# Attention with the transposes of the probabilities one head later, three probability buffers, and a loop over three groups

## The reference

```
q = (x @ Wq.T).reshape(B, L, HQ, HD)        # HQ, HKV, HD = 32, 8, 64; L = 512
k = (x @ Wk.T).reshape(B, L, HKV, HD)
v = (x @ Wv.T).reshape(B, L, HKV, HD)
q, k = _rope(q), _rope(k)                   # rotation of pairs of features by the position
attn = einsum('bkgqd,bkld->bkgql', qh, kh) * HD ** -0.5
p = softmax(where(causal, attn, -inf), axis=-1)
out = einsum('bkgql,bkld->bkgqd', p, vh)
x = x + out.reshape(B, L, HQ * HD) @ Wo.T
```

## Time and profile before

| | |
|---|---|
| median of 3 runs | 1674.26 us (1673.71 to 1676.47) |
| the profiled execution | 1673.25 us |
| its span, first to last instruction | 1671.5 us |
| PE busy | 1508.4 us (90%) |
| DVE busy | 1381.9 us (83%) |
| ACT busy | 1116.1 us (67%) |
| POOL busy | 1050.1 us (63%) |
| mean granted TensorE clock | 0.942 of full speed |

### The profile page before, as it was taken

The page is one execution under the profiler, slowest core; times in us unless marked ns, Lnnn a source line. Parts: engine busy times, 40 slices in busy tenths (PEclk is TensorE's granted clock), DMA queues, the critical chain, the costliest instruction groups (busy, mean ns, idle before and its releaser), DMA issues. The chain is left out here.

```text
span 1671.5 us, 31714 instructions
## 1 busy us (share of the span) xinstructions
PE 1508.4 (90%) x8951; PEld 1317.9 (79%) x8951; DVE 1381.9 (83%) x3470; ACT 1116.1 (67%) x2593; POOL 1050.1 (63%) x1161
## 2 busy tenths in 40 slices
PE   5799999999999899899899999698679999999994
PEld 4687877887778788788788878587569999999993
DVE  7898898898898898898888888377668898899882
ACT  3787877787777788788778778432146666666661
POOL 6689779779769769778778877556613322322321
PEclk9999999999999999999999999856579999999997
DMA  4000000000000000000000000111368888888775
GB/s 172 1 14 20 1 14 20 1 13 19 1 13 19 1 13 19 1 13 19 1 13 0 1 1 1 40 58 64 104 222 227 225 230 225 227 234 219 197 182 132
DMA packets 62002, 124.47 MB, mean 74 GB/s; under 512 B 20942, under 2 KB 21070, under 8 KB 61792
## 3 DMA queue, kind: packets, MB, share of 16 engines
q1 hardware_dynamic: 51408, 102.24, 19.3%
q0 software_dynamic: 10304, 20.59, 6.5%
q10 hardware_dynamic: 144, 0.07, 0.0%
HBM read 106.08 MB, written 24.71 MB: 78 GB/s over the span
## 5 line engine op out<-in xcount | busy, mean ns | idle before, releaser
L522 POOL TENSOR_SCALAR probs<-probs,row_inv 128x512 f32<-128x512 f32 (+3 forms) x512 | 282.3, 572 | 25.6 <-DVE row_inv L426 25.6
L306 ACT ACTIVATE probs<-probs,neg_max 128x512 f32<-128x512 f32 (+3 forms) x512 | 281.5, 552 | 10.2 <-DVE neg_max L419 6.5
L419 DVE CUSTOM_DVE_ANT_0 probs<-bank,causal 128x512 f32<-128x512 f32 (+3 forms) x512 | 220.6, 485 | 55.4 <-PE bank L208 42.1
L1209 POOL DMA_INDIRECT acc<-ctx_raw,idx x46 | 74.5, 1618 | 294.2 <-ACT ctx_raw L1362 279.9
L218 PE MATMUL bank<-ident,probs 128*128 128x128 f32 x1280 | 187.1, 277 | 55.5 <-POOL probs L522 38.0
L407 DVE TENSOR_TENSOR pt_lo<-bank,pt_hi 128x512 fp32r<-128x512 f32 (+1 forms) x384 | 214.8, 585 | 22.8 <-ACT pt_hi L299 22.7
L218 PEld LDWEIGHTS bank<-ident,probs 128*128 128x128 f32 x1280 | 149.8, 141 | 103.4 <-issue 48.0
L513 POOL TENSOR_TENSOR rot<-rot,sin 128x512 f32<-128x512 f32 (+1 forms) x96 | 124.0, 1291 | 165.2 <-DVE rot L438 161.8
L1290 PE MATMUL bank<-xt_hi,gu_hi 128*128 128x256 f32 x736 | 208.0, 283 | 2.0 <-DVE xt_lo L407 1.5
L1290 PE MATMUL bank<-xt_hi,gu_lo 128*128 128x256 f32 x736 | 206.2, 280 | 0.0
L1290 PE MATMUL bank<-xt_lo,gu_hi 128*128 128x256 f32 x736 | 206.2, 280 | 0.0
(11 more groups left out here) (204 smaller groups left out, 4188.5 us busy)
## 6 DMA issues: line engine op xcount, KB each, us to landing
gu_raw<-in_gate_up SPq DMA_DIRECT2D x92, 512.0 KB, 3.9
dn_raw<-in_down SPq DMA_DIRECT2D x92, 256.0 KB, 3.6
w_raw<-in_wqkv SPq DMA_DIRECT2D x8, 768.0 KB, 4.4
w_raw<-in_wo_rows SPq DMA_DIRECT2D x8, 512.0 KB, 3.5
h_rows<-ln_h SPq DMA_DIRECT2D x16, 256.0 KB, 2.0
acc<-x_res SPq DMA_DIRECT2D x4, 1024.0 KB, 4.6
x_res<-in_x SPq DMA_DIRECT2D x3, 1024.0 KB, 11.2
ctx_raw<-in_ctx SPq DMA_DIRECT2D x2, 512.0 KB, 6.8
```

The source lines that it names most:

```text
L306: nc.scalar.activation(row, row, ACT.Exp, bias=neg_max[:, hb, i:i + 1], scale=-1.0, accum_out=row_sum[:, hb, i:i + 1]).then_inc(s["exp_don ...
L419: nc.vector.tensor_tensor_reduce(out=probs[:, hb, P_AT[i]:P_AT[i] + (i + 1) * P], in0=S_BANK[k][:, at:at + (i + 1) * P], in1=causal[:, (QB ...
L522: nc.gpsimd.tensor_scalar(row, row, row_inv[:, hb, i:i + 1], 0.0, ALU.mult, ALU.add).then_inc(s["pnorm_done"], 1)
```

## The change

Everything from the transposes of the probabilities on (transposes, pt_hi and pt_lo, the product with v, o_part, the sum, o_hi and o_lo, the output projection, its addition, and the split of Wo) runs one step later than before, for d = c - 1 instead of c, with db, dh, dn_ and dm as its batch, head, number and batch number. Scores, mask, exponentials, normalization, projections, rotation, q_lo, k_lo and v stay with c. Group 7 gets a 17th step for the last head. probs, neg_max, row_sum and row_inv have three buffers in place of two, chosen by (r + c) % 3, where r is the group's number modulo 3 (16 steps shift the buffer by one). The loop body is three groups long and runs twice, so r is a constant in each group. wo_out has two tiles in place of four (ScalarE waits for an addition two tiles back rather than four), and o_part and v_t are the two halves of one tensor. act_group is changed in the same way as the others. The diff, cut to its core:

```diff
@@ -135,22 +135,22 @@
         cos = sa("cos", [P, L])
         sin = sa("sin", [P, L])
         causal = sa("causal", [P, L])
-        probs = sa("probs", [P, 2, P_LEN])
+        probs = sa("probs", [P, 3, P_LEN])
         pt = [[sa(f"pt{b}_hi", [P, PT_LEN], F32R), sa(f"pt{b}_lo", [P, PT_LEN], F32R)] for b in range(2)]
         q_st = sa("q_st", [P, G, L], F32R)
         k_hi = sa("k_hi", [P, 2, L], F32R)
         k_lo = sa("k_lo", [P, 2, L], F32R)
-        v_t = sa("v_t", [HD, L])
         v_st = sa("v_st", [P, 2, QB, P], F32R)
         rot = sa("rot", [P, L])
         rope = sa("rope", [P, 2, L])
-        wo_out = sa("wo_out", [P, QB, D])
-        o_part = sa("o_part", [HD, L])
+        wo_out = sa("wo_out", [P, 2, D])
+        v_and_o = sa("v_and_o", [P, L])
+        o_part, v_t = v_and_o[0:HD, :], v_and_o[HD:P, :]
         o_f = sa("o_f", [P, L])
         o_st = [sa("o_hi", [P, 4, L], F32R), sa("o_lo", [P, 4, L], F32R)]
-        neg_max = sa("neg_max", [P, 2, QB])
-        row_sum = sa("row_sum", [P, 2, QB])
-        row_inv = sa("row_inv", [P, 2, QB])
+        neg_max = sa("neg_max", [P, 3, QB])
+        row_sum = sa("row_sum", [P, 3, QB])
+        row_inv = sa("row_inv", [P, 3, QB])
         ln_out = probs
 
...
@@ -249,21 +249,27 @@
                     first = False
             last.then_inc(s["wo_done"], 1)
 
-        def pe_group(pe, g):
-
-
-
-
-            for c in range(HEADS):
+        def pe_group(pe, g, r):
+
+
+
+
+            for c in range(HEADS + (isinstance(g, int) and g == GROUPS - 1)):
                 b, h = divmod(c, G)
                 n, m = HEADS * g + c, B * g + b
+                front = c < HEADS
                 begun = not (isinstance(g, int) and g == 0 and c == 0)
-                more = not (isinstance(g, int) and g == GROUPS - 1 and c == HEADS - 1)
-                next_batch = not (isinstance(g, int) and g == GROUPS - 1 and b == B - 1)
-                last_batch = not (isinstance(g, int) and g == 0 and b == 0)
-                batch_before_last = not (isinstance(g, int) and g == 0 and b < 2)
-                if begun:
-                    pe_ptrans(pe, n - 1, (c + 1) % 2, 2)
+                more = not (isinstance(g, int) and g == GROUPS - 1 and c >= HEADS - 1)
+                next_batch = not (isinstance(g, int) and g == GROUPS - 1 and b >= B - 1)
+                d = c - 1
+                db, dh = divmod(d, G)
+                dn_, dm = HEADS * g + d, B * g + db
+                d_here = not (isinstance(g, int) and g == 0 and d < 0)
+                d_begun = not (isinstance(g, int) and g == 0 and d < 1)
+                d_last = not (isinstance(g, int) and g == 0 and db < 1)
+                d_before_last = not (isinstance(g, int) and g == 0 and db < 2)
+                if d_begun:
+                    pe_ptrans(pe, dn_ - 1, (r + d - 1) % 3, 2)
                 if more:
                     pe_scores(pe, n + 1, m if h < G - 1 else m + 1, (h + 1) % G, (b + (h == G - 1)) % 2)
                 if h < 3 and b == 3 and next_batch:
@@ -281,18 +287,19 @@
                 if h == 3 and next_batch:
                     pe.wait_ge(s["rope_in"], 3 * m + 6)
                     pe_vt(pe, m + 1)
-                if h == 3 and last_batch:
-                    pe_wo(pe, m - 1, (b - 1) % 2, 2)
-                pe_ptrans(pe, n, c % 2, 0)
-                pe_ptrans(pe, n, c % 2, 1)
-                if begun:
-                    pe_pv(pe, n - 1, m if h else m - 1, (c + 1) % 2, (b if h else b + 1) % 2)
-                if h in (1, 2) and last_batch:
-                    if h == 1 and b == 1:
+                if dh == 3 and d_last:
+                    pe_wo(pe, dm - 1, (db - 1) % 2, 2)
+                if d_here:
+                    pe_ptrans(pe, dn_, (r + d) % 3, 0)
+                    pe_ptrans(pe, dn_, (r + d) % 3, 1)
+                if d_begun:
+                    pe_pv(pe, dn_ - 1, dm if dh else dm - 1, (d + 1) % 2, (db if dh else db + 1) % 2)
+                if dh in (1, 2) and d_last:
+                    if dh == 1 and db == 1:
                         pe.wait_ge(s["w2_lo_done"], 2 * g + 2)
-                    pe_wo(pe, m - 1, (b - 1) % 2, h - 1)
-                if h == 0 and batch_before_last:
-                    pe_wo(pe, m - 2, b % 2, 3)
+                    pe_wo(pe, dm - 1, (db - 1) % 2, dh - 1)
+                if dh == 0 and d_before_last:
+                    pe_wo(pe, dm - 2, db % 2, 3)
 
 
...
         def act_wo(act, m, t, src=WO_BANK):
 
             act.wait_ge(s["wo_done"], 4 * m + t + 1)
-            wait(act, s["woacc_done"], 4 * m + t - 3)
-            nc.scalar.activation(wo_out[:, t, :], src[:, :], ACT.Copy).then_inc(s["wo_out_done"], 1)
-
...
@@ -409,7 +424,7 @@
         def dve_masked(dve, n, hb):
 
 
-            wait(dve, s["ptrans_done"], 3 * n - 3)
+            wait(dve, s["ptrans_done"], 3 * n - 6)
             for i in (3, 2, 1, 0):
                 k = (2, 2, 1, 0)[i]
...
-        def dve_group(dve, g):
-
-            for c in range(HEADS):
+        def dve_group(dve, g, r):
+
+            for c in range(HEADS + (isinstance(g, int) and g == GROUPS - 1)):
                 b, h = divmod(c, G)
                 n, m = HEADS * g + c, B * g + b
+                front = c < HEADS
                 begun = not (isinstance(g, int) and g == 0 and c == 0)
-                more = not (isinstance(g, int) and g == GROUPS - 1 and c == HEADS - 1)
-                next_batch = not (isinstance(g, int) and g == GROUPS - 1 and b == B - 1)
+                more = not (isinstance(g, int) and g == GROUPS - 1 and c >= HEADS - 1)
+                next_batch = not (isinstance(g, int) and g == GROUPS - 1 and b >= B - 1)
+                d = c - 1
+                db, dh = divmod(d, G)
+                dn_, dm = HEADS * g + d, B * g + db
+                d_here = not (isinstance(g, int) and g == 0 and d < 0)
+                d_begun = not (isinstance(g, int) and g == 0 and d < 1)
+                d_last = not (isinstance(g, int) and g == 0 and db < 1)
+                d_before_last = not (isinstance(g, int) and g == 0 and db < 2)
                 if more:
-                    dve_masked(dve, n + 1, (c + 1) % 2)
-                if begun:
-                    dve_pt(dve, n - 1, (c + 1) % 2, 2)
-                if begun and h % 2 == 1 and c > 0 and not (isinstance(g, int) and g == 0 and c == 1):
-                    dve_o(dve, HEADS // 2 * g + (c - 1) // 2 - 1, ((c - 1) // 2 - 1) % 4)
-                if h == 0 and begun:
+                    dve_masked(dve, n + 1, (r + c + 1) % 3)
+                if d_begun:
+                    dve_pt(dve, dn_ - 1, (d + 1) % 2, 2)
+                if d_begun and dh % 2 == 1 and not (isinstance(g, int) and g == 0 and d == 1):
+                    dve_o(dve, HEADS // 2 * g + (d - 1) // 2 - 1, ((d - 1) // 2 - 1) % 4)
+                if h == 0 and begun and front:
                     dve_q_lo(dve, m, 2, b % 2)
                 if h == 2 and next_batch:
                     dve_q_lo(dve, m + 1, 1, (b + 1) % 2)
-                if h == 1 and b == 1:
+                if dh == 1 and db == 1:
                     dve_w2(dve, g)
                 if h < 3 and next_batch:
                     dve_rope_in(dve, m + 1, h, (b + 1) % 2)
                 if more:
-                    dve_recip(dve, n + 1, (c + 1) % 2)
-                dve_pt(dve, n, c % 2, 0)
-                dve_pt(dve, n, c % 2, 1)
+                    dve_recip(dve, n + 1, (r + c + 1) % 3)
+                if d_here:
+                    dve_pt(dve, dn_, d % 2, 0)
+                    dve_pt(dve, dn_, d % 2, 1)
                 if h == 3 and next_batch:
                     dve_v(dve, m + 1, (b + 1) % 2)
-                if begun:
-                    dve_oadd(dve, n - 1, (c - 1) % 2, HEADS // 2 * g + ((c - 1) // 2 if c else -1))
+                if d_begun:
+                    dve_oadd(dve, dn_ - 1, (d - 1) % 2, HEADS // 2 * g + (d - 1) // 2)
 
 
         def pool_rope(pool, m, r, mb):
...
             wait(pool, s["pnorm_done"], 16 * m - 8)
-            wait(pool, s["woacc_done"], 4 * m - 8)
+            wait(pool, s["woacc_done"], 4 * m - 9)
             for half_ in range(2):
...
             pool.wait_ge(s["wo_out_done"], 4 * m + t + 1)
             tile = x_res[:, b * QB + t, :]
-            nc.gpsimd.tensor_tensor(tile, wo_out[:, t, :], tile, ALU.add).then_inc(s["woacc_done"], 1)
-
...
                 if h == 1 and next_batch:
                     pool_k_lo(pool, m + 1, (b + 1) % 2)
                 if h < 3 and next_batch:
                     pool_rope(pool, m + 1, h, (b + 1) % 2)
-                if not (isinstance(g, int) and g == GROUPS - 1 and c == HEADS - 1):
-                    pool_norm(pool, n + 1, (c + 1) % 2)
-                if h and last_batch:
-                    pool_woacc(pool, m - 1, (b - 1) % B, h - 1)
-                if h == 0 and not (isinstance(g, int) and g == 0 and b < 2):
-                    pool_woacc(pool, m - 2, (b - 2) % B, 3)
+                if more:
```

(61 more changed lines are left out.)

62 lines of the change are left out of this document (34 added, 28 removed).

## The result

| | before | after |
|---|---|---|
| median | 1673.99 us (4 runs) | 1659.97 us (1659.38 to 1664.38, 4 runs) |
| the profiled execution | 1673.25 us, span 1671.5 | 1664.38 us, span 1662.6 |
| mean granted TensorE clock in it | 0.942 | 0.941 |

The change makes the kernel faster: ratio 0.9924 with a 95% interval of 0.9907 to 0.9940, some 13 us. I had forecast 33 us (1640). The time lies in my range; the size of the gain does not hold. The profiled execution of after is the slowest of its four runs, so I compare the attention stage and no totals. Its last matmul of an output projection starts at 1072.69 us before and at 1062.62 now: 10.1 us earlier.

What follows compares the result with a forecast made beforehand. TensorE, 90% busy, was taken to lose time in attention mostly waiting for GpSimd's probabilities and at back edges. Back edges 8.3, plus 26 for the shift, minus 1.5 for the drain gave 33 us: 1673.25 to 1640 us, range 1615 to 1668.

Steps and rivals of the forecast that it cites:

- at h = 2 above all: Sign at the opening transposes: TensorE newly waits for pt_lo, mostly at h = 2, 0.3 to 1.5 us each.
- The back edges: Attention loop: one back edge instead of five, four saved at 2.07 us each, 8.3 us.
- The wait for the probabilities goes entirely: TensorE's transposes: the 34.8 us wait for GpSimd's normalized probabilities vanishes, as long as GpSimd keeps up.
- h = 0 at 7.9, h = 2 at 8.5: Head lengths in us, with o_lo and q_lo now in the same heads on VectorE, delaying pt_lo.
- VectorE becomes the bound: Rival: GpSimd work meets o_lo and q_lo in both even heads, 9.3 us each; slower, 1705 us; 11%.
- The split of Wo: VectorE's split moves from h = 1 to h = 2; TensorE's output projection waits, 2.5 us more per group.
- h = 1 and 3 are at the floor: 7.81 and 5.7: Heads that lost o_lo on VectorE take only TensorE's own time, 7.81 and 5.7 us.
- The splits of the projection weights: GpSimd's splits delay it into the next h = 0: 0 to 1.8 us, taken as 0.6 per group.
- The first and the last group as one and a half: Groups outside the loop, with fewer stalls, counted as 1.5 groups at 3.5 us saved each.
- the drain: Extra round without scores at the end: a third 1.5 us wait for pt_lo, -1.5 us of gain.
- Only the back edges count: Rival: the wait for GpSimd becomes an equal wait for pt_lo; 3 us gained, 1670 us, halfway 1655; 20%.
- TensorE at its floor: Rival: o_lo and q_lo hide everywhere, h = 2 takes 7.81, a group 119; 61 us gained, 1612 us; 15%.

Runs made afterwards that it cites:

- e3: Kernel before with only the loop body made three groups long (two turns, one back edge); 1668.92 us, ratio 0.9962 to before.
- e2: Kernel before with the output projection of h = 3 moved from ahead of the eight transposes to behind the product with v; 1683.19 us, ratio 1.0052 to before.
- e1: Kernel after with an output projection put back ahead of the transposes of h = 3; 1654.22 us, ratio 0.9888 to before.
- e5: Kernel after with the output projection back ahead of h = 3's transposes and the projection-weight splits on VectorE; 1638.43 us, ratio 0.9780 to before.
- e4: Kernel after with its three projection-weight splits per group moved from GpSimd to VectorE; 1647.19 us, ratio 0.9832 to before.

## Why the prediction was off

The sign was right, and so was the first half of the mechanism: the wait for the probabilities goes, and a wait for VectorE's pt_lo comes in its place. Where that wait comes, and why, was not, and the gain was 2.5 times too large. Of my signs the new waits for pt_lo "at h = 2 above all" failed. By the steps of the prediction:

- *The back edges*, 8.3 us: right, at the upper end (6.4, 4.2 to 8.4, by e3). I had added up the late heads at the edges, 12.0 us. But the five groups that begin with an edge are only 9.5 us longer together than the first one (126.59): part of each loss is made up within the group.
- *The wait for the probabilities goes entirely*: right, 34.8 to 3.1 us; three waits are left, all in the last group (from 953 us on).
- *h = 0 at 7.9, h = 2 at 8.5*: better than that, 7.77 and 7.80, apart from the steps 6, 12 and 14. I had put 0.7 us on h = 2 for a meeting of q_lo and an addition. The addition comes 0.2 us after q_lo instead. h = 2 took 33.8 us per group where I had 36.5, and this error hid more than half of the one at h = 3. The rule from the Trainium skill that I weighed (page "SBUF — State Buffer", section "Who interferes with whom") says that a VectorE instruction with two inputs in SBUF and a GpSimd instruction that reads SBUF shut each other out. The trace agrees where they meet: 3.06 us for o_lo beside an addition and a split, 0.87 for half of q_lo beside the normalization. But only step 12 is a place where it costs much, so the rival "VectorE becomes the bound" fell.
- *The split of Wo*, 2.5 us: right, 9.97 - 7.80 = 2.2. (The lower end of its bounds, 1.7, doesn't follow from my own 9.5 to 11.8, which give 1.0 to 3.3; the term is the same.)
- *h = 1 and 3 are at the floor: 7.81 and 5.7*: **this step failed**, for h = 3. 6.72 to 6.89 instead of 5.7 is 4.5 us per group, more than the whole gain of 3.5 that I had for a group. I had taken 5.68 from a row of before as TensorE's own time. It was that only since an output projection stood between pt_lo and the transposes that need it. Six matmuls with a spacing of 0.23 us are 1.4 us of cover; without them 1.06 us is waited. The diff shows the line: `h == 3` became `dh == 3`. I had listed the output projection as moved, with a wrong place for it at h = 3, and priced no cover. e2 makes the same wait in the kernel before; e1 takes it away in after. It is not all that lacked: with the filler back a group still takes 124.7 us, since ScalarE's o_hi holds up h = 0 and GpSimd's splits step 12. With the splits moved as well (e5) it takes 121.7, one less than my 122.7, and the kernel 1638 us, where I had 1640.
- *The splits of the projection weights*, 0.6 us: mis-sized. 2.1 us per group by e4, since at one place two instructions of GpSimd follow each other directly and o_lo waits for both.
- *The first and the last group as one and a half*, +5.3 us, and *the drain*, -1.5 us: wrong in sign together. The loop begins 2.8 us later than before (173.57 against 170.76), and behind the loop attention takes 135.5 us (927.10 to 1062.62) against 132.9 (939.83 to 1072.69). Together -5.5 us where I had +3.8. Some 2 of these 5.5 belong to the clock of that one execution and not to the change, as shown below.

TensorE's openings at the end show the drain. First after, then before:

```profile
1027.24 0.44 PE L218 MATMUL bank<-ident,probs 128*128 128x128 f32 x2 [0.79 <-DVE pt_lo L422]
...
1034.45 0.38 PE L218 MATMUL bank<-ident,probs 128*128 128x128 f32 x2
...
1041.22 0.38 PE L218 MATMUL bank<-ident,probs 128*128 128x128 f32 x2
...
1046.46 0.38 PE L218 MATMUL bank<-ident,probs 128*128 128x128 f32 x2
```
```profile
1042.96 0.38 PE L218 MATMUL bank<-ident,probs 128*128 128x128 f32 x2
...
1049.73 0.38 PE L218 MATMUL bank<-ident,probs 128*128 128x128 f32 x2
...
1056.50 0.39 PE L218 MATMUL bank<-ident,probs 128*128 128x128 f32 x2
```

From the last of these rows on both kernels take 16.2 us, with the same waits. The round between 1041.22 and 1046.46 is the one that was added. It is not a wait but a whole round of 5.24 us, since without projections the last heads run at the pace of the chain (6.8 us each) and not at TensorE's. I had counted one wait of it. At the start TensorE waits 12.2 us for pt_lo up to 173 us, nine times, the longest 3.82 us at 65.00, where before it waited 6.5 for probs and 2.4 for pt_lo: the pipeline has one more stage to fill. But little of it is lost, as the kernels e1 and e4 show, which are the same as after up to step 6. Step 5 opens at 85.92 us in before, at 85.97 and 85.94 in e1 and e4, and at 87.99 in the profiled execution of after. The 2 us in between go with the granted clock of that execution: from 50 to 55 us it was 0.64, where e1 and e4 had 0.91 and before 0.83, and from 65 to 70 us it was 0.50 (1.2 GHz, the lower level, with 0.63 us for a 512-column matmul), where e1 and e4 had 0.70 and 0.71 and before 1.00. TensorE had waited 3.7 to 3.8 us just before the second stretch in the three shifted kernels. A difference of this size comes without the change too: in e3, whose first group is that of before, the loop begins at 172.79, 2.0 us later than in before. So the cost of the fill is not shown to differ from nothing. At the end it is different. From the loop to the last output projection before and e3 take 132.9 and 132.7 us, after and e4 135.5 and 134.4, and both of these have the added round, 5.24 and 5.23. No experiment took the drain apart; this reading is from the traces alone.

The sum of what was measured, at the end of the attention stage: the loop gave 15.5 us (769.07 to 753.53). Of these the longer body alone gives 6.9 (762.13 in e3), which leaves 8.6 for the shift in six groups, 1.4 each where I had 3.5. What lies before and behind the loop took 5.5 back, some 2 of it by the clock: 10.1 us. The forecast had 8.3, 21 and 3.8 = 33.

Between the rivals, "Only the back edges count" (3 us, up to 18 halfway) came nearest in time, but not by its mechanism: it put the new wait for pt_lo at h = 0 and h = 2, and it came at h = 3. "TensorE at its floor" held for h = 0, 1 and 2 outside the steps 6, 12 and 14.

## What to carry to other kernels

When half of a software pipeline is moved by one step, the fillers that move with it matter as much as the chain that is relaxed: for each short step, list what stood between a producer and its consumer on the bound engine, before and after. A head's length in the old trace is a floor only with the cover that it had there. Putting a filler back gives little as long as the next engine in the chain is late by almost as much (6 us alone here, 22 together with the splits). In this kernel the deeper pipeline paid a whole round at its end, not one wait.
